# Running maxima of a graph attention layer kept in PSUM banks instead of SBUF

## What is computed

```
h = x @ W_node.T                      # 3125 x 64
hi = h @ a_node[:D];  hj = h @ a_node[D:]
e_n = leaky(hi[i_idx] + hj[j_idx])    # slope 0.05, edges and loops
alpha_n = segment_softmax(e_n, i_idx, N)   # subtracts the maximum of each segment
x_from_nodes = scatter_mean(alpha_n[:, None] * h[j_idx], i_idx, N)
```

## Time and profile before the change

| | us |
|---|---|
| median of 3 runs | 3286.65 |
| lowest, highest | 3284.67, 3296.16 |
| the profiled execution | 3289.45 |
| its span | 3287.7 |
| busy: TensorE, VectorE, ScalarE, GpSimd | 1828.8, 2188.0, 763.6, 1626.0 |

### The profile page before, as it was taken

One profiled execution on the slowest core, in us unless ns is written; L12 is line 12 of the kernel. 1 busy time (PEld: TensorE's weight loads), 2 busy tenths in 40 slices (PEclk: granted clock), 3 DMA queues, 4 the chain that ended last, 5 costly groups with the idle time before them and its releaser, 6 DMA issues. The chain is left out here.

```text
span 3287.7 us, 42891 instructions
## 1 busy us (share of the span) xinstructions
PE 1828.8 (56%) x12299; PEld 1264.3 (38%) x12299; DVE 2188.0 (67%) x4651; ACT 763.6 (23%) x2054; POOL 1626.0 (49%) x1520
## 2 busy tenths in 40 slices
PE   4333312215666555299925841395017889965994
PEld 3222211113444333277724731143012258853652
DVE  6766646627777876577776954104859966657996
ACT  0010101102222222133311001001008845522341
POOL 0777767727777777177664775600850025510000
PEclk9999999997676776555557975697559999967997
DMA  8555596588877777988804840381936636615760
GB/s 323 169 166 163 177 245 193 166 61 225 229 228 227 225 229 211 53 201 203 197 1 111 190 92 0 125 306 72 408 143 240 231 91 129 129 35 144 200 188 29
DMA packets 706541, 555.06 MB, mean 169 GB/s; under 512 B 392348, under 2 KB 651996, under 8 KB 694054
## 3 DMA queue, kind: packets, MB, share of 16 engines
q1 hardware_dynamic: 647572, 449.82, 52.1%
q0 software_dynamic: 58752, 102.49, 8.9%
HBM read 371.29 MB, written 180.85 MB: 168 GB/s over the span
## 5 line engine op out<-in xcount | busy, mean ns | idle before, releaser
L1327 POOL DMA_INDIRECT table<-pay_own,stage x432 | 450.1, 1042 | 279.4 <-issue 121.7
L598 POOL DMA_INDIRECT adjacency<-gm_slot,slot_tmp x440 | 449.3, 1021 | 216.0 <-issue 134.9
L1327 POOL DMA_INDIRECT table<-q,stage x424 | 446.0, 1052 | 134.2 <-issue 119.2
L1533 PE MATMUL banks<-pool,both 128*128 x1320 | 261.1, 368 | 180.5 <-ACT pay_own L1543 74.3
L1289 PE MATMUL banks<-acc,work 128*128 128x26 bf16 (+1 forms) x856 | 82.5, 226 | 487.5 <-DVE work L1283 487.1
L1261 DVE TENSOR_SCALAR work<-acc,pidx 128x512 bf16<-128x512 bf16 x214 | 81.2, 380 | 351.5 <-DMA acc<-low_rows_by_src 202.5
L2229 POOL TENSOR_TENSOR pool<-pool,raw 128x260 f32<-128x260 f32 x110 | 115.1, 1047 | 353.3 <-DMA pool<-table 244.7
L1289 PEld LDWEIGHTS banks<-acc,work 128*128 128x128 bf16 x856 | 44.2, 110 | 556.7 <-DVE work L1283 555.4
L1533 PEld LDWEIGHTS banks<-pool,both 128*128 128x128 bf16 x1320 | 159.5, 121 | 252.8 <-issue 196.9
L1279 ACT CAST work<-banks 128x104 bf16<-128x104 f32 x214 | 59.2, 277 | 658.2 <-PE banks L1271 652.5
L450 PE MATMUL banks<-q,both 128*128 x1320 | 171.8, 295 | 0.1
(11 more groups left out here) (496 smaller groups left out, 4681.7 us busy)
## 6 DMA issues: line engine op xcount, KB each, us to landing
work<-adjacency SPq DMA_DIRECT2D x75, 1600.0 KB, 6.7
adjacency<-slots SPq DMA_DIRECT2D x100, 400.0 KB
acc<-table SPq DMA_DIRECT2D x110, 332.0 KB
q<-table SPq DMA_DIRECT2D x110, 256.0 KB
pool<-table SPq DMA_DIRECT2D x220, 128.0 KB, 2.3
table<-slots SPq DMA_DIRECT2D x16, 1320.0 KB, 23.2
work<-adjacency SPq DMA_DIRECT2D x25, 832.0 KB
work<-adjacency SPq DMA_DIRECT2D x25, 768.0 KB
```

Source lines behind the costliest of these rows:

```text
L598: nc.gpsimd.indirect_dma_start(adjacency, bass.IndirectOffsetOnAxis(ap=pair_at[:, t:t + 1], axis=0), pair_n[:, t:t + 1], None).then_inc(co ...
L1327: nc.gpsimd.indirect_dma_start(to, bass.IndirectOffsetOnAxis(ap=stage[n % 4][:, j:j + 1], axis=0), pay[n % 4][:, j, 0:width], None).then_i ...
L1533: last = nc.tensor.matmul(kv_of[j], rohT[n % 2][:, j, :], kv16[:, bass.ds(blocks[j], 1), part, :].rearrange("p o d -> p (o d)"), start=par ...
```

## The change

The running maxima are kept in the first 3200 float32 columns of PSUM (`peaks = banks[:, 0:NPAD]`, banks 0 to 6, the last one a quarter full) in place of `peaks2` in SBUF. L1946 and L1949 write `peaks`, and L1949 reads it. When all 25 steps are done, ScalarE copies the banks one by one into `peaks2` (seven copies), and TensorE's transposes wait for the copy of their own bank, in place of one wait for the 25 steps. What the transposes read, and where they write, stays as it was. GpSimd's and SyncE's lists are not changed.

```diff
+            peaks = banks[:, 0:NPAD]
...
                         if b == 0:
-                            ins = nc.vector.tensor_scalar(peaks2, cells[0], scale2[:, 0:1], None, ALU.min)
+                            ins = nc.vector.tensor_scalar(peaks, cells[0], scale2[:, 0:1], None, ALU.min)
                         else:
                             v.wait_ge(s_u, b)
-                            ins = nc.vector.scalar_tensor_tensor(out=peaks2, in0=cells[b % 3], scalar=scale2[:, b:b + 1],
-                                                                 in1=peaks2, op0=ALU.min, op1=ALU.max)
+                            ins = nc.vector.scalar_tensor_tensor(out=peaks, in0=cells[b % 3], scalar=scale2[:, b:b + 1],
+                                                                 in1=peaks, op0=ALU.min, op1=ALU.max)
...
-                    pe.wait_ge(s_u, NB)
                     for b in range(NB):
+                        pe.wait_ge(s_k, b // 4 + 1)
                         last = nc.tensor.transpose(ps[b // 4][:, (b % 4) * P:(b % 4 + 1) * P], peaks2[:, b * P:(b + 1) * P], ident[:, :])
...
                 @block.scalar
                 def _(act):
+                    act.wait_ge(s_u, NB)
+                    for c in range(7):
+                        n = min(512, NPAD - c * 512)
+                        nc.scalar.copy(peaks2[:, c * 512:c * 512 + n], ps[c][:, 0:n]).then_inc(s_k, 1)
```

More of the change, by code:

```diff
@@ L1898, in neighbour_maxima @@
         def neighbour_maxima():
-            s_v, s_p, s_u, s_t, s_r, s_c, s_rw = (sem(f"maxima_{k}") for k in (
-                "chain", "products", "blocks_done", "turned", "reduced", "rows_copied", "rows_written"))
+            s_v, s_p, s_u, s_k, s_t, s_r, s_c, s_rw = (sem(f"maxima_{k}") for k in (
+                "chain", "products", "blocks_done", "peaks_kept", "turned", "reduced", "rows_copied", "rows_written"))
+            peaks = banks[:, 0:NPAD]
             s_ld = [sem(f"maxima_cells_loaded{k}") for k in range(3)]
```

## The result

| | us |
|---|---|
| before, median of 5 runs | 3290.59 (3284.67 to 3296.16) |
| changed, median of 5 runs | 3269.05 (3268.13 to 3275.20) |
| ratio | 0.9939, 95% interval 0.9922 to 0.9956 |
| profiled execution of the change, its span | 3268.13, 3266.3 |

The kernel is faster by 0.6%: the medians are 21.5 us apart, where 23.9 us and 3263 were forecast.

What follows compares the result with a forecast made beforehand. GpSimd's held scatters were taken to end the maxima block at 2441.53 us; with crowding 0.6, copies 0.65 and the tail it would end at 2417.6, 23.9 less: 3286.65 - 23.9 = 3262.7, forecast 3263, 8-in-10 range 3257 to 3282.

Steps and rivals of the forecast that it cites:

- (f): Block's tail: first row write at 2415.6, then 1.7 us for SyncE and 0.3 handover; block ends at 2417.6, 23.9 us less.
- (a): GpSimd's 50 scatters: no longer held, 1.26 us apart, done at 2371.0, so GpSimd leaves the path with about 39 us spare.
- (b): VectorE's 24 maxima in PSUM: 3.55 us each, bounds 3.54 and 6.88; anything up to 3.81 us is hidden by the loads.
- half rate: Rival, chance 0.08: PSUM steps take 6.88 us and become the bound; block ends 50 us later, 3337 us.
- mild surcharge: Rival, chance 0.08: PSUM steps take 3.85 to 4.6 us, costing 1 to 19 us of the 24; 3264 to 3282 us.
- (c): First maximum, L1946: loses its double rate, 2.02 to 3.55 us; cost 0, or 1.5 us if the cover by queued loads fails.
- the cover: First maximum: two loads still queued, 3.85 us each, were to hide the 1.5 us later release of the first buffer.
- VectorE makes the delay good from its 0.3 us a step: First maximum: VectorE's spare 0.3 us in each step was to recover the later start within about five steps.
- (d): Scatters crowding into the loads: 22 more at 0.026 us of DMA time each, 0.6 us taken, lower bound 0; last maximum 2406.5.
- 2308 to 2314 window: Trace before: loads ran at 431 GB/s with scatters at the free pitch, taken as evidence for a lower bound of 0.
- (e): ScalarE's seven copies: transposes wait for the first, +0.65 us, the other six hidden; bounds 0.6 to 2 us.
- forecast's own range: Whole kernel: 3258 to 3269 us, from margins on the first maximum, crowding and copies plus 3 us either side for run spread.

Runs made afterwards that it cites:

- e2: Changed kernel with the running maxima alternating between PSUM and SBUF from step to step; block 123.2 us, last scatter started at 91.0 us.
- e6: Kernel before, maxima in SBUF, with the first maximum in a slower two-input form (3.55 us); 3281.79 us in one run.
- e3: Changed kernel with GpSimd waiting for all 25 steps before its scatters; last maximum at 107.56 us, block 178.46 us.
- e9: Changed kernel with the first maximum written to SBUF and all scatters behind the last step; 3323.79 us in one run, block 173.7 us.
- e1: The changed kernel run once more with no edit; last maximum at 110.42 us, block 121.46 us.
- e5: Changed kernel with the first maximum written to SBUF and read there by the second step; 3262.54 us in one run, block 118.55 us.
- e11: The changed kernel measured again on another chip; median 3265.20 us, ratio to the kernel before 0.9943, block 120.89 us.
- e4: Kernel before, maxima in SBUF, with GpSimd waiting for all 25 steps before its scatters; last maximum at 102.95 us, block 174.29 us.
- e10: Kernel before with all scatters behind the last step, a second time on another chip; last maximum at 102.93 us, block 174.14 us.

## Why the prediction was right, and where its sum was off

- *What bounds the kernel.* Right: GpSimd ended the block. Freed of it, the block ends 2.08 us behind SyncE's first row write; 2.0 was forecast in (f).
- *(a) Scatters.* Right: 50 at 1.26 us, the last starts at 2364.5 on a block that began 5.5 us earlier, 67.2 us from its start, where the forecast has (2308.0 + 49 x 1.26) - 2302.8 = 66.9. That the second SBUF input is the cause was argued from the tensor-reduce in the earlier trace rows; e2 shows it with the very instruction. The rule of the Trainium skill (SBUF — State Buffer, Who interferes with whom) on instructions with at most one SBUF input agrees: 0.96 us under such a step. It leaves out the 2-port performance modes, a condition that the prediction dropped; the 2.14 us scatter under the one-input L1946 at double rate fits it, though no run shows that L1946 is in such a mode. The section's inferred exception for tensor_tensor does not agree, by the tensor-tensor instructions in the earlier trace rows; e2 shows the hold with a scalar-tensor-tensor whose output is in PSUM.
- *(b) Steps in PSUM.* Right: 3.555 us, where 3.55 was taken, within bounds of 3.54 and 6.88. The half rate and the mild surcharge did not occur. The skill's extra 65 ns (Perfetto Trace Analysis, Optimizing Scalar/DVE Operations) is not seen here: the difference is 4 ns.
- *(c) First maximum.* Its duration was right, 3.55. Its cost was not: put at 0 with 1.5 us as the bound, it is 1.5 us for the step and 0.5 (e6, without its dip) to three us more in slower loads (e3). The first failed step is the cover. When the first buffer is released, 11.9 us from the block's start, not two loads are still queued but the rest of one: by 12 us the three loads have brought 369 GB/s x 12 us = 4.4 of their 4.9 MB. In e3, with no scatters, the rate falls to 269 GB/s at a share of 0.81 between 13 and 14 us; in e9, where the release comes at 10.2 us, it is 422. The second failed step is "VectorE makes the delay good from its 0.3 us a step". That 0.3 is VectorE's slack, not the loads'. The loads are the bound, and the late release of a buffer is time that they lose; nothing gives it back. In the stretch from 12 to 20 us they run at 367 GB/s instead of 416.
- *(d) Crowding.* Put at 0.6 us with 0 as the lower bound; 2.6 to 2.9 beside the late release (after and e1 against e3), 4.4 without it (e5 against e9). The failed step is the pricing by share of the DMA engines, 0.026 us a scatter. That share was right: with scatters at the free pitch it is 1.9% from 20 to 60 us, 0.02 us for each. What the sum lacked are the two dips of about 2 us each, in which the loads run at 241 and 274 GB/s at a share of 0.92 and 1.00. Three of the four scatters of the 2308 to 2314 window were at the free pitch (the fourth is the 2.14 us one), and its 431 GB/s was right for the time beside scatters; but the window ended long before the first dip.
- *(e) Copies.* The first row write comes 8.79 us behind the last maximum; the forecast was 8.46 + 0.65 = 9.11. The seven copies take 3.20 us, 0.52 for each full one, and the transposes start 0.67 us behind the last maximum. Here the sum was 0.3 us too high in this profile. The first row write varies by more from run to run: 8.58 to 9.36 us behind the last maximum in the ten with the copies, 8.12 to 8.46 in the four without.
- *The sum.* Forecast 23.9; the block shows 138.71 - 121.00 = 17.7. The difference is 6.5 (load phase, 7.1 against 0.6) - 0.3 (copies) + 0.1 (handover), but for rounding. The measured median, 3269, lies in the range; it is at the edge of what was called the forecast's own range, 3258 to 3269, whose terms for (c) and (d) were too small. That the medians came as near as 21.5 us to 23.9 is in part luck: two more runs had moved the median before from 3286.65 to 3290.59, and on the chip of e11 they are 18.9 us apart. Two slips in the working changed nothing: the terms as given make the lower edge 3259 (3263 - 0.6 - 3), and the middle of 3264 to 3282 is 3273, not 3271.

What is left open: what causes a dip 4.5 to 9.5 us behind the 25th and the 50th scatter, and why the waits of a late release come again at many steps in e3 and not in e6. The runs show when the loads slow down and what moves that time, not what happens in the queues. No run changed the number of scatters in a row, so it is not shown whether the count, the end of a set or something else sets off the dip.

## What to carry to other kernels

When GpSimd issues indirect DMAs beside long VectorE instructions, look at the durations of its rows under each form of instruction: one with two tensors in SBUF held it for the whole 3.5 us, one with a tensor in SBUF and the other in PSUM did not, at the same speed for VectorE; a one-input instruction at double rate in SBUF held it as well, 2.14 us. When loads are the bound, a consumer's slack is no reserve: what counts is how early each buffer is released, so price a slower first step in full. Price company on the DMA engines by the loads' GB/s in windows laid over its whole course and some 10 us beyond, not by its share: here the price came in two short dips behind it. After such a change look for the bound that takes over; here it was answered with two more buffers, loads issued a block earlier and the fast first step kept, another 0.4%.

## What the runs showed of the hardware that was not expected

- A VectorE instruction that reads and writes the same 3200 float32 columns over seven PSUM banks takes 3.555 us, against 3.551 with both in SBUF (after).
- A tensor-scalar that runs at double rate from SBUF to SBUF (1.89 us in e4, e9 and e10, 2.02 before and in e5) takes 3.55 us with its output in PSUM (after). At double rate it holds a scatter of GpSimd, 2.14 us (before, e5), though it has one input.
- Loads that ran at 405 to 427 GB/s fell to 220 to 302 GB/s for 5 us, beginning 4.5 us behind the end of the 25th and of the 50th scatter, in 17 cases in nine runs, at a DMA share of 0.92 to 1.02. The busy share does not show them.
- With a late release of the first of three buffers and no scatter beside them, the loads ran at 349 GB/s at a share of 0.92 from 12 to 20 us (e3), against 416 at 1.00 (e9).
